# State space of a mixed decoder: GpSimd adds the squares of two chunks, tail decays from the decays' last columns, late decays issued ahead of the result

## What is computed

```python
zxbcdt = x @ in_w.T                       # z 256, xBC 512, dt 4
y = conv1d(xBC, 4 taps, depthwise);  xBC = silu(y + conv_b)
dt = softplus(dt + dt_bias);  A = -exp(A_log)
xh = xs.reshape(b, l, H_SSM, HEADDIM)
y = ssd(xh * dt[..., None], A * dt, Bh, Ch, CHUNK)
y = y + D[None, None, :, None] * xh
y = rmsnorm(y * silu(z), norm_w)          # mean of squares over the 256 features
return y @ out_w.T

# ssd: Acs = cumsum(A*dt); within reach of a chunk  C_l . B_s * exp(Acs_l - Acs_s) * x_s  for s <= l,
# and across chunks the same product through a state, decayed by exp(Acs_end - Acs) and exp(Acs)
```

## Time and profile before

| what | value |
|---|---|
| median of 3 runs | 2397.5 us (2397.4 to 2401.65) |
| profiled execution: its time, its span | 2397.09 us, 2395.1 us |
| PE, DVE, ACT, POOL busy over the span | 81%, 67%, 55%, 28% |
| mean granted TensorE clock | 0.906 of full |
| state space stage, from about | 563 to 1024 us |
| PE, DVE, ACT, POOL busy from 563 to 1024 us | 425.79, 288.66, 334.37, 145.13 us of 461.00 |
| granted clock in that stretch | 0.99 |

### The profile page before, as it was taken

One profiled execution on the slowest core, in us unless ns is written; L12 is line 12 of the kernel. 1 busy time (PEld: TensorE's weight loads), 2 busy tenths in 40 slices (PEclk: granted clock), 3 DMA queues, 4 the chain that ended last, 5 costly groups with the idle time before them and its releaser, 6 DMA issues.

```text
span 2395.1 us, 38613 instructions
## 1 busy us (share of the span) xinstructions
PE 1937.9 (81%) x13680; PEld 1308.3 (55%) x13680; DVE 1605.2 (67%) x3738; ACT 1310.2 (55%) x2684; POOL 676.9 (28%) x631
## 2 busy tenths in 40 slices
PE   6999775988999999867875188898887898668796
PEld 4666562446777777732443064555555577424464
DVE  6778675766666666547848946787778556658543
ACT  4666532766777777624755336666666312337632
POOL 2112003203332233314004533555555101031033
PEclk9999986998999999977998598999999898869897
DMA  4000004411000000006301000000000100154022
GB/s 184 1 1 1 1 1 119 131 34 36 1 1 1 1 1 1 1 16 177 91 1 72 0 1 1 1 1 1 1 1 1 45 9 1 65 174 133 16 58 76
DMA packets 80014, 87.44 MB, mean 37 GB/s; under 512 B 6562, under 2 KB 70099, under 8 KB 78801
## 3 DMA queue, kind: packets, MB, share of 16 engines
q1 hardware_dynamic: 78481, 82.49, 11.1%
q0 software_dynamic: 1344, 2.49, 0.4%
HBM read 54.39 MB, written 30.70 MB: 36 GB/s over the span
## 4 chain that ended last, share of the span: by engine, by line
PE 45%; DVE 22%; issue 15%; POOL 10%; ACT 6%; DMA 2%; SPq 0%; POOLq 0%; DVEq 0%; ACTq 0%
PE bank L469 39%; POOL w_early L3294 3%; DVE scratch L1226 3%; POOL scratch L3289 3%; POOL scratch L3294 2%; DVE w_keep L1927 2%; PE bank L653 1%; PE bank L368 1%; DVE stats L245 1%; POOL w_early L3281 1%; PE bank L693 1%; DVE scratch L721 1%; PE bank L1195 1%; DVE w_early L2539 1%; ACT w_keep L1312 1%
## 5 line engine op out<-in xcount | busy, mean ns | idle before, releaser
L469 PE MATMUL bank<-scratch 64*128 64x256 bf16 (+7 forms) x3056 | 337.9, 308 | 75.7 <-DMA scratch<-parts 39.5
L1226 DVE TENSOR_REDUCE scratch<-bank 128x2 f32<-128x512 f32 x384 | 245.5, 685 | 98.4 <-PE bank L469 95.6
L469 PEld LDWEIGHTS bank<-scratch 64*128 64x128 bf16 (+4 forms) x3056 | 185.9, 123 | 198.2 <-DVE scratch L1226 65.2
L469 PE MATMUL bank<-w_keep,scratch 128*128 128x128 f32 (+4 forms) x1760 | 252.3, 336 | 35.6 <-ACT scratch L806 20.8
L1312 ACT ACTIVATE w_keep<-bank 128x512 f32<-128x512 f32 x384 | 210.7, 596 | 70.3 <-PE bank L469 64.6
L469 PEld LDWEIGHTS bank<-w_keep,scratch 128*128 128x128 f32 (+3 forms) x1760 | 188.3, 188 | 99.0 <-issue 49.0
L469 PE MATMUL bank<-XNT,w_keep 128*128 128x256 f32 (+4 forms) x800 | 236.1, 434 | 6.8 <-POOL w_keep L2175 4.6
L469 PE MATMUL bank<-w_early,scratch 64*128 64x256 f32 (+3 forms) x1152 | 172.4, 360 | 44.2 <-ACT w_early L3192 25.8
L469 PEld LDWEIGHTS bank<-XNT,w_keep 128*128 128x128 f32 x800 | 148.9, 196 | 59.2 <-issue 30.3
L469 PEld LDWEIGHTS bank<-w_early,scratch 64*128 64x128 f32 (+3 forms) x1152 | 123.0, 190 | 95.8 <-issue 37.4
L806 ACT ACTIVATE scratch<-bank,scratch 128x256 f32<-128x256 f32 x256 | 100.5, 475 | 77.3 <-DVE scratch L721 77.3
(11 more groups left out here) (458 smaller groups left out, 4116.7 us busy)
## 6 DMA issues: line engine op xcount, KB each, us to landing
scratch<-parts SPq DMA_DIRECT2D x24, 1024.0 KB, 5.0
parts<-scratch SPq DMA_DIRECT2D x192, 96.0 KB, 2.4
parts<-scratch SPq DMA_DIRECT2D x96, 64.0 KB, 2.1
w_early<-pack_l3f SPq DMA_DIRECT2D x1, 5206.0 KB, 16.0
w_keep<-pack_l2f SPq DMA_DIRECT2D x1, 2124.0 KB, 13.0
w_early<-pack_mamba SPq DMA_DIRECT2D x1, 2120.0 KB, 19.0
w_keep<-pack_l2x SPq DMA_DIRECT2D x1, 2049.0 KB, 8.3
w_keep<-taps SPq DMA_DIRECT2D x4, 512.0 KB, 5.5
```

The costliest lines, as they stand in the source:

```text
L469: return pe.matmul(out, lhsT, rhs, start=start, stop=stop, skip_group_check=True)
L1226: dve.tensor_reduce(neg[:, :, h], self.k.bank[5 - g % 2][:, :].rearrange("p (t s) -> p t s", s=S), AXX, ALU.max, negate=True).then_inc(*s. ...
```

## The change

Four edits, all in `StateSpace`.

1. ScalarE's squares of a unit (256 features as two groups of 128 columns by token) are added group to group by one new GpSimd instruction (`squares_pool`), behind the weights multiply of each iteration. The mean on TensorE then takes two matmuls per unit in place of four, and waits for GpSimd instead of ScalarE.
2. The 128x4 matmul of the tail sums is gone. The tail decays are the exponential of the last column of each head's decays in bank 5, made by a new 128x4 ScalarE instruction ahead of decay 0.
3. Late matmuls move from the start of TensorE's iteration to behind the second part of the convolution, ahead of the result; the late exponential of a unit is made at the same place of ScalarE's list, one iteration later.
4. Off moves from bank 2 to bank 0, where it takes turns with raw.

```diff
@@ late_bank, raw_bank
-        uses = [("late", n - 1, s.weighed, "late"), ("root", n - 5, s.lowered, "root"), ("out", n - 5, s.added, "final"), ("off", n - 2, s.normed, "off")]
+        uses = [("root", n - 5, s.lowered, "root"), ("out", n - 5, s.added, "final"), ("late", n - 1, s.weighed, "late")]
+        return [x for x in uses if there(x[1])]
+
+    def raw_bank(self, n):
+
+        s, there = self.k.s, lambda u: 0 <= u < UNITS
+        uses = [("raw", n, s.stacked, "raw"), ("off", n - 2, s.normed, "off")]
         return [x for x in uses if there(x[1])]
@@ raw_pe
-        if u >= 1:
-            pe.wait_ge(*s.stacked.at("raw", u - 1))
+        self.freed(pe, self.raw_bank, u, "raw")
@@ late_pe
-            mm(pe, bank[rows, cols], a3[:, 1, h:h + 1].to_broadcast([P, HP]), self.upto)
-        mm(pe, bank[:, S:S + H_SSM], self.k.w["after"], a3[:, 0, :]).then_inc(*s.scored.up("late", u))
+            m = mm(pe, bank[rows, cols], a3[:, 1, h:h + 1].to_broadcast([P, HP]), self.upto)
+        m.then_inc(*s.scored.up("late", u))
@@ result_pe
-        self.freed(pe, self.late_bank, u + 2, "off")
+        self.freed(pe, self.raw_bank, u + 2, "off")
         for c in range(INNER):
-            m = mm(pe, late[:, c * P:(c + 1) * P], self.xu[u % 2][:, c * P:(c + 1) * P], self.gm[u % 2][:, 2 * P:3 * P])
+            m = mm(pe, off[:, c * P:(c + 1) * P], self.xu[u % 2][:, c * P:(c + 1) * P], self.gm[u % 2][:, 2 * P:3 * P])
@@ mean_pe
-        pe.wait_ge(*s.flip_s.at("sq", u + j))
+        pe.wait_ge(*s.pool.at("sq", u + j))
...
-            for c in range(INNER):
-                m = mm(pe, bank[:, at:at + 1], self.two(self.sq[(u + j) % 2])[:, c, t * P:(t + 1) * P], self.k.w["ones"][:, 0:1], c == 0, c == INNER - 1)
+            m = mm(pe, bank[:, at:at + 1], self.sq[(u + j) % 2][:, t * P:(t + 1) * P], self.k.w["ones"][:, 0:1])
@@ pe
             if there(prep):
-                self.late_pe(pe, prep)
                 self.decay_pe(pe, prep, 0)
...
                 self.convolve_pe(pe, conv, 1)
+            if there(prep):
+                self.late_pe(pe, prep)
             if there(heads):
                 self.result_pe(pe, heads)
@@ late_act, decay_act
-            act.wait_ge(*s.pool.at("xu", u - 2))
-        act.activation(self.late[u % 2], self.k.bank[2][:, 0:S + H_SSM], ACT.Exp).then_inc(*s.weighed.up("late", u))
+        act.activation(self.late[u % 2][:, 0:S], self.k.bank[2][:, 0:S], ACT.Exp).then_inc(*s.weighed.up("late", u))
...
+        if t == 0:
+            if u >= 2:
+                act.wait_ge(*s.pool.at("xu", u - 2))
+            ends = columns_of(self.k.bank[5][:, :], P - 1, (P, H_SSM))
+            act.activation(self.late[u % 2][:, S:S + H_SSM], ends, ACT.Exp)
@@ act
+            if there(n - 2):
+                self.late_act(act, n - 2)
             if there(prep):
-                self.late_act(act, prep)
                 self.decay_act(act, prep, 0)
@@ middle_pool
-        pool.wait_ge(*s.weighed.at("late", u))
+        pool.wait_ge(*s.weighed.at("decay", u, 0))
@@ squares_pool, pool
+    def squares_pool(self, pool, u):
+
+        s, sq = self.k.s, self.sq[u % 2]
+        pool.wait_ge(*s.flip_s.at("sq", u))
+        pool.tensor_tensor(sq[:, 0:S], sq[:, 0:S], sq[:, S:2 * S], ALU.add).then_inc(*s.pool.up("sq", u))
...
                 self.weights_pool(pool, prep)
+            if there(n - 3):
+                self.squares_pool(pool, n - 3)
```

More of the change, by code:

```diff
@@ L1799, in result_pe @@
     def result_pe(self, pe, u):
-        s, out, late, xd, wt = self.k.s, self.k.bank[7], self.k.bank[2], self.xd[u % 2], self.by_head(self.wt[u % 2])
+        s, out, off, xd, wt = self.k.s, self.k.bank[7], self.k.bank[0], self.xd[u % 2], self.by_head(self.wt[u % 2])
         pe.wait_ge(*s.formed.at("xd", u))
@@ L1969, in sums_dve @@
         dve.wait_ge(*s.summed.at("off", u))
-        dve.tensor_tensor(self.off[u % 2], self.k.bank[2][:, 0:S], self.late[u % 2][:, 0:S], ALU.mult).then_inc(*s.normed.up("off", u))
+        dve.tensor_tensor(self.off[u % 2], self.k.bank[0][:, 0:S], self.late[u % 2][:, 0:S], ALU.mult).then_inc(*s.normed.up("off", u))
     def mean_dve(self, dve, u):
```

## The result

| | before | changed |
|---|---|---|
| median, runs | 2397.45 us (2396.98 to 2401.65, 4 runs) | 2425.66 us (2424.51 to 2433.29, 4 runs) |
| ratio, 95% interval | | 1.0118 (1.0105 to 1.013) |
| span of the profiled execution | 2395.1 us | 2422.7 us |
| mean granted TensorE clock | 0.906 | 0.900 |

The change costs 28 us. The direction was forecast; the size, 12.6 us, was less than half, and the result lies above the range.

A forecast was written before the change was run, and what follows sets the result against it. A chain of waits over TensorE, VectorE and ScalarE, not TensorE alone, was taken to set the 28.81 us period. Loop +10.5, ramp -1.5 and tail +3.6 gave +12.6 on 2397.1: 2410 us, range 2404 to 2414.

The forecast's parts named there:

- rival (c): TensorE's granted clock falls behind longer idle: +1.7 us per period, 2432 us, or 2415 to 2420 if only some fall; chance 0.11.
- Part 3: Late moved behind the second convolution: odd half 0.36 us shorter, even half 0.60 longer as late waits for the final multiply.
- Even part: Second half of the two-iteration period, 13.66 us before: forecast 0.60 us longer from late's wait and 0.57 from GpSimd's add.
- the hold: GpSimd's longer stretch holds a VectorE multiply ahead of the softplus series: 0.57 us longer in the even half.
- odd part: First half of the two-iteration period, 15.15 us before: forecast 0.36 us shorter, with root waiting for the late exponential.
- Part 4: GpSimd adds the squares, holding VectorE's L1602: 0.57 us longer in the even half, bounds 0 and 0.61.
- The loop's sum without the clock: Per period of two iterations -0.36 + 0.60 + 0.57 = +0.81 us; 13 periods from n = 6 to 30 give +10.5.
- Ramp: Iterations before the steady loop: late and the 128x4 matmul leave the path twice, the mean shortens, the series loses 0.57: -1.5 us.
- Tail: Last iterations: y behind final and late +1.9, table load and exponential between square root and root +1.5, squares +0.2: +3.6 us.
- Parts 1 and 2: On TensorE, mean matmuls halved (0.81 to about 0.41 us) and the 128x4 matmul gone (0.25 less in each half).
- Rival (b): TensorE alone closes the loop, so only removed matmuls count: 13 x 0.65 = 8.5 us less, 2389 us; chance 0.10.
- Rival (a): GpSimd's add of the squares costs VectorE nothing: 13 x 0.57 + 0.57 less than forecast, 2402 us; chance 0.13.

The follow-up runs named there:

- e7: The changed kernel with no edit, run on another chip: 2423.89 us beside 2398.85 for the kernel before, ratio 1.0104.
- e4: Changed kernel plus four useless 128x256 matmuls in the idle ahead of late, even iterations 6 to 30: 2399.77 us, 1.0041 to the kernel before.
- e3: Changed kernel with GpSimd's add of squares held until VectorE's tap next to the last is done: 2392.4 us, 1.0014 to the kernel before.
- e2: Changed kernel with the squares summed on TensorE again, four matmuls per unit, no GpSimd add: 2393.57 us, 1.0016 to the kernel before.
- e1: Changed kernel with late matmuls moved behind gate instead of ahead of y: 2405.63 us, 1.0062 to the kernel before.
- e10: Changed kernel with late behind gate, squares on TensorE, last late exponential at the end of ScalarE's n = 32, no useless matmuls: 2401.65 us, 1.0049.
- e5: Changed kernel with the moves of e1 and e3 together: 2405.19 us, 1.0037 to the kernel before.
- e6: e5 plus four useless 128x256 matmuls ahead of root in odd iterations 7 to 31: 2394.78 us, 0.9985 to the kernel before.
- e8: e6 with the last late exponential made at the end of ScalarE's iteration 32: 2397.2 us, 0.9992 to the kernel before.
- e9: e8 with the useless matmuls starting at n = 5: 2378.84 us, 0.9957 to the kernel before.

## Why the prediction was wrong

The idle time of TensorE in one place of the loop, and the clock behind it, over all kernels (13 periods, n = 6 to 30):

| kernel | idle before late / before the odd root, us | falls in the loop | ratio |
|---|---|---|---|
| before | 0.66 (before off) / 1.36 | none | 1 |
| changed, and again in e7 | 2.06 / 1.76 | 10 of 13 | 1.0118, 1.0104 |
| e4 | 0.34 / 1.76 | none | 1.0041 |
| e3 | 1.59 / 1.76 | none | 1.0014 |
| e2 | 1.60 / 1.31 | none | 1.0016 |
| e1 | none / 2.81 | 10 of 13 | 1.0062 |
| e10 | none / 2.18 | 10 of 13 | 1.0049 |
| e5 | none / 2.06 | 6 of 13 | 1.0037 |
| e6, e8, e9 | none / 0.33 | none | 0.9985, 0.9992, 0.9957 |

1. **The step that failed: the sum has no term for the granted clock.** The fall stood only in rival (c), which was given 0.11, with the words that the clock held behind 2.12 us at 583.57. One row of the ramp, behind a different idle pattern, was no bound for a loop that repeats it 13 times. Ten periods fell, each for 1.61 (forecast 1.7), 16.1 us of 28. With the rival's own price on ten of 13 periods the forecast would have been 2427; that this is near 2425.7 is partly luck, since other terms were off both ways (points 4 to 6). The mechanism and the price were in the text; the sum took the clock as constant all the same. The Trainium skill (TensorE: Matmul & The Clock Gate, HAM oscillation) was cited beside it for falls caused by repeated idle between groups of matmuls: the runs agree in kind, e6 against e5 above all, though not every period fell (ten of 13, and six in e5).
2. **Part 3, the queue behind late's wait.** Right in kind: late waits for the final multiply with y, off, turn and gate behind it. Too dear: late's block takes 0.49 without the 128x4 matmul behind it, the hand-over 0.06 and not 0.14, and late to the end of gate 3.31 and not 3.46. Even part +0.93 with the hold (forecast +1.17), odd part -0.50 (forecast -0.36).
3. **Part 4, the hold.** 0.48 for 0.57, between the bounds, and on L1604 and not L1602. The Trainium skill (SBUF — State Buffer, Who interferes with whom) says that the order of issue decides; the trace agrees, since L1602 was issued (658.41) before the add (659.32), and L1604 (659.42) behind it. e2 and e3 show the hold by its absence.
4. **The loop's sum without the clock** was +0.81 a period and measured +0.43: 12 x 0.38 = 4.6 us too much from n = 6 to 30. This error went against the one on the clock and hid part of it: 16.1 for the clock, -4.6 here, 1.8 for the ramp, 1.1 for the thirteenth period and the tail, and 0.7 from outside the stage make the 15 us of span that the forecast lacks.
5. **Ramp.** Forecast -1.5, measured +0.3. The waits before late went as said (1.96 us gained up to n = 4, though TensorE now waits 1.42 and 2.01 us for ScalarE's `early` copies ahead of decay 0), but a half-clock stretch that lay on work with slack moved onto root and the convolution. The same step failed: work was priced and the clock was not.
6. **Tail.** Forecast +3.6 and 0.81 for the thirteenth period, measured +5.5 for both, 1.1 more. Both mechanisms are there; the square-root one is 1.28 + 0.38, and e8 got 1.15 back within the stage. The clock's fall at 1032.1 has no term either: the two rows on it take 1.57 us longer than before. That it makes up the 1.1 is an estimate from these rows; no run took it away alone.
7. **Parts 1 and 2** are a gain once late stands behind gate and the add is held back: 28.14 for 28.81, 0.67 a period, as TensorE's removed work gives (0.65). Rival (b)'s size was right for another order of the same work. Rival (a) fell with e2 and e3.

Open: what exactly makes the clock fall. The table is what stood in these loops, and no rule: idle of 1.76 us or less in one place went with the full level in every period of these loops, and 2.06 or more with a fall in many but not all; what the 64-row and one-column matmuls near the gap add to it was not separated. The length of one gap can't be all of it: in the ramp of the kernel before the clock fell at 609.5, and the idle ahead of that was only this:

```profile
608.69 0.66 PE L469 MATMUL bank<-w_keep,scratch 128*64 128x128 f32 x8 [1.16 <-DVE scratch L1970]
```

e10's 2.18 was misjudged by 0.3 as well. And all totals carry a scatter of some microseconds from chip and from other stages, so e8 is not told from e6.

## What to carry to other kernels

Where an edit lengthens an idle gap of TensorE in a loop, cost the gap twice: once as a wait, and once as the granted clock behind it over what is queued there; look in the trace of before for the longest gap in that loop that kept the full level, and price anything clearly above it both ways (here 1.36 was the longest before, 1.76 still kept it, 2.06 lost it in six to ten of 13 periods). Filling the gap with work that nobody reads can then win time. That removing work from TensorE ahead of such a wait can lose time follows from this, but no run shows it alone. And where an edit puts a wait into an in-order queue, put it behind the work that doesn't need it: late behind gate and the add behind VectorE's series turned a period of 29.24 into one of 28.14. It also gathered the idle in one place, 2.06 us ahead of root, and only with that filled did the loop gain.

## What the hardware showed that was not expected

- Four useless matmuls per period made the kernel 10 us faster (e5 to e6, 2405.19 to 2394.78, on one chip), by 2.06 us of idle turned to 0.33.
- Equal gaps are not followed by equal clocks: 2.07 at 663.72 kept it, 2.06 at 785.50 did not, and so in e5.
- In the changed kernel half a microsecond on VectorE (the hold) decided whether TensorE ran at the half clock for 3.4 us in most periods of 31 (2.06 us of idle with it, 1.59 without it in e3).
